# Router logits, a token transposition and an output product cut to the column tiles of the matmuls around them

## The reference

```python
h = _L0_tok_ref(x)
h = h + _L0_attn_ref(_layernorm(h), Wq, Wk, Wv, Wo)
h = h + _L0_ffn_ref(_layernorm(h), sW1, ..., gW, gb)

def _L0_attn_ref(q_input, Wq, Wk, Wv, Wo):        # 8 heads of 64
    qkt = jnp.einsum('bifh,bjfh->bijh', q, k)
    attn = jax.nn.sigmoid(qkt * SCALE)
    wv = jnp.einsum('bijh,bjfh->bifh', attn, v)
    return jax.nn.relu(wv.reshape(b * s, f * h) @ Wo)

def _L0_ffn_ref(x, ...):                            # 4 experts, the best 2 of each token
    all_out = _experts_mlp(x, eW1, eb1, eW2, eb2, eW3, eb3)
    shared = _shared_mlp(x, sW1, sb1, sW2, sb2, sW3, sb3)
    gates = jax.nn.softmax(x @ gW + gb, axis=-1)    # the router
    topv, topi = jax.lax.top_k(gates, TOPK)
    topw = jax.nn.softmax(topv, axis=-1)
    ...
```

## Time and profile before

| | |
|---|---|
| runs | 157.02, 158.77, 161.1 us; median 158.77 |
| the profiled execution | 158.76 us, of which the span from first to last instruction is 156.9 |
| busy share of the span | PE 93%, PEld 56%, DVE 71%, ACT 76%, POOL 35% |
| first and last scores of the part that matters | 81.38 us (step 48), 98.09 us (step 63) |

### The profile page before, as it was taken

How to read it: one execution, slowest core, us unless ns; L and a number is a source line. 1 busy time by engine, 2 the same in 40 slices (tenths; PEclk the granted TensorE clock), 3 DMA queues, 4 the chain that set the end, 5 groups by cost and what they waited for, 6 DMA issues and landing times.

```text
span 156.9 us, 6708 instructions
## 1 busy us (share of the span) xinstructions
PE 146.5 (93%) x2856; PEld 87.3 (56%) x2856; DVE 111.0 (71%) x282; ACT 119.3 (76%) x163; POOL 55.4 (35%) x102
## 2 busy tenths in 40 slices
PE   7999595998999999999999999999999999999990
PEld 2479532544456665656665656453566476576680
DVE  2396998998676958586763253879568987879680
ACT  3498992886888999999997989779738767857530
POOL 7000008879498473738265316376100000000000
PEclk9999659999999999999999999999999999999999
DMA  4390000156687496689589800101000010000112
GB/s 107 72 279 24 4 0 0 34 140 188 171 231 209 158 293 138 196 199 258 148 254 176 169 5 4 33 13 24 6 4 18 19 37 19 20 21 16 39 37 65
DMA packets 16734, 15.02 MB, mean 96 GB/s; under 512 B 4792, under 2 KB 15964, under 8 KB 16640
## 3 DMA queue, kind: packets, MB, share of 16 engines
q1 hardware_dynamic: 15888, 13.97, 34.0%
q10 hardware_dynamic: 816, 0.62, 1.3%
HBM read 9.06 MB, written 4.60 MB: 87 GB/s over the span
## 4 chain that ended last, share of the span: by engine, by line
PE 73%; DVE 7%; DMA 6%; ACT 6%; POOL 4%; issue 1%; POOLq 0%; DVEq 0%
PE ps L487 15%; PE ps L505 14%; PE ps L618 9%; PE ps L634 9%; PE ps L516 5%; DMA y_stage<-YP 4%; PE ps L676 4%; PE ps L644 3%; DMA YS<-y_stage 2%; PE ps L368 2%; PE ps L698 2%; PE ps L721 2%; PE ps L357 2%; PE ps L542 2%; POOL norm L1426 1%
## 5 line engine op out<-in xcount | busy, mean ns | idle before, releaser
L1315 ACT ACTIVATE probs<-ps 125x1000 f32<-125x1000 f32 x64 | 63.1, 1006 | 7.7 <-PE ps L487 3.3
L505 PE MATMUL ps<-probs,xn 124*32 124x250 f32 (+1 forms) x512 | 38.5, 375 | 0.3 <-ACT probs L1315 0.3
L487 PE MATMUL ps<-YS,XT 128*32 128x500 f16 x448 | 33.8, 375 | 1.1 <-DMA YS<-y_stage 1.1
L1333 ACT ACTIVATE area<-ps,wf 128x500 f32<-128x500 f32 x32 | 21.1, 672 | 7.7 <-PE ps L618 7.7
L940 DVE COPY ZS<-ps 128x250 f32<-128x250 f32 x32 | 13.2, 413 | 16.9 <-PE ps L505 16.9
L505 PEld LDWEIGHTS ps<-probs,xn 124*32 124x32 f32 (+1 forms) x512 | 15.3, 109 | 12.6 <-ACT probs L1315 1.2
L1347 ACT ACTIVATE area<-ps,wf 128x500 f32<-128x500 f32 x20 | 13.5, 676 | 4.7 <-PE ps L644 2.4
L634 PE MATMUL ps<-area,wf 128*64 128x500 f32 x64 | 16.3, 584 | 0.0
L516 PEld LDWEIGHTS ps<-outW,ZS 128*32 128x32 f32 (+1 forms) x512 | 10.7, 108 | 5.0 <-issue 0.6
L487 PEld LDWEIGHTS ps<-YS,XT 128*32 128x32 f16 x448 | 10.0, 96 | 5.5 <-DMA YS<-y_stage 2.1
L921 DVE CAST YP<-ps 128x500 f16<-128x500 f32 x14 | 9.5, 677 | 4.5 <-PE ps L446 4.1
(11 more groups left out here) (170 smaller groups left out, 263.2 us busy)
## 6 DMA issues: line engine op xcount, KB each, us to landing
YS<-y_stage SPq DMA_DIRECT2D x28, 250.0 KB, 4.2
y_stage<-YP SPq DMA_DIRECT2D x10, 250.0 KB, 3.8
wf<-wf_in SPq DMA_DIRECT2D x1, 648.0 KB, 5.8
y_stage<-YP SPq DMA_DIRECT2D x5, 125.0 KB, 4.6
tower_out<-res SPq DMA_DIRECT2D x5, 124.0 KB
wa<-wa_in SPq DMA_DIRECT2D x1, 512.0 KB, 5.1
y_stage<-YP ACTq DMA_DIRECT2D x3, 125.0 KB, 2.9
tower_out<-res SPq DMA_DIRECT2D x2, 112.0 KB
```

The lines of the kernel that those rows point to most:

```text
L487: last = mm(ps[k0:k1, 2 * (n % 2) + j, 0:TG].rearrange("p (h n) -> p h n", h=2), XT[:, g % 3, (2 * bb + cj) * P + k0:(2 * bb + cj) * P + k ...
L505: last = mm(ps[R * hh:R * hh + R, 4 + bb, half * TB:(half + 1) * TB], xn[0:keys, 4 * g + 2 * bb + cj, :], probs[0:keys, n % 3, hh, :], sta ...
L1315: fn(probs[:, n % 3].rearrange("p (j h) n -> p j (h n)", j=2), ps[0:P, 2 * (n % 2):2 * (n % 2) + 2, 0:TG], ACT.Sigmoid, scale=SCORE_SCALE) ...
L1333: fn(H1[:, g % 2, e, :], ps[:, n % 3, 0:TG], ACT.Relu, bias=wf[:, WF["b1"][0] + e:WF["b1"][0] + e + 1]).then_inc(l1_act, 1)
```

## The change

Four edits. The router's matmuls are cut along the token columns: tiles of 32 columns in the first router, of 64 in the second. The first router goes in eight pieces of two token tiles, behind steps 0, 1, 2, 7 of group 6 and 0, 1, 4, 7 of group 7. The transposition of the last group's tokens is cut in two 64-column parts for each token tile in the place of four of 32. Group 1's output product goes one token tile a step (t = 4 to 7). On DVE, `gate_logits(0)` moves behind `z_take(7, 2)`, since its input is now complete only in step 63.

```diff
-GATE_STEPS = tuple(8 * (NG - 2) + t for t in (0, 1, 2, 7))
+GATE_STEPS = tuple(8 * (NG - 2) + t for t in (0, 1, 2, 7, 8, 9, 12, 15))
...
-                    for c in range(4):
-                        last = nc.tensor.transpose(xt[R * c:R * c + R, i, 0:P], x2s[0:P, g % 2, i, R * c:R * c + R],
+                    for c in range(2):
+                        last = nc.tensor.transpose(xt[F * c:F * c + F, i, 0:P], x2s[0:P, g % 2, i, F * c:F * c + F],
...
-                    row = NB * r + i
-                    last = mm(ps[0:P, bank, 2 * i * E:2 * (i + 1) * E],
-                              X2T[:, row // 4, row % 4, 0:P],
-                              wg[:].rearrange("p k e -> p (k e)"), start=True, stop=True)
+                    row, wide = NB * r + i, F if r else R
+                    for q0 in range(0, P, wide):
+                        q1 = min(q0 + wide, P)
+                        last = mm(ps[q0:q1, bank, 2 * i * E:2 * (i + 1) * E],
+                                  X2T[:, row // 4, row % 4, q0:q1],
+                                  wg[:].rearrange("p k e -> p (k e)"), start=True, stop=True)
...
-                return {1: (6, 7), NG - 2: (3, 4, 5, 6), NG - 1: (2, 3, 5, 6)}.get(g, (3, 5, 6, 7))
+                return {1: (4, 5, 6, 7), NG - 2: (3, 4, 5, 6), NG - 1: (2, 3, 5, 6)}.get(g, (3, 5, 6, 7))
...
-                    first_tile = out_steps(g).index(t) * 4 // len(out_steps(g))
-                    if first_tile == 0 and g + 2 < NG:
+                    tile = out_steps(g).index(t)
+                    if tile == 0 and g + 2 < NG:
                         pe.wait_ge(xt_cp, g + 3)
-                    elif first_tile == 0:
+                    elif tile == 0:
                         pe.wait_ge(h2_done, g - 1)
-                    attn_out(g - 1, range(first_tile, first_tile + 4 // len(out_steps(g))))
+                    attn_out(g - 1, (tile,))
                 if n in GATE_STEPS:
                     i = GATE_STEPS.index(n)
-                    gates(0, slice(4 * i, 4 * i + 4))
+                    gates(0, slice(2 * i, 2 * i + 2))
...
                 z_take(g, 1)
                 if g == NG - 1:
-                    gate_logits(0)
                     add_attention(g - 1)
                     centre2(g - 1)
                 z_take(g, 2)
+                if g == NG - 1:
+                    gate_logits(0)
```

## The result

Over 22 runs the changed kernel takes 156.75 us (154.59 to 159.64), the kernel before 158.87 (157.02 to 161.56, 22 runs). The ratio is 0.985, 95% interval 0.981 to 0.988. That is faster, by less than the 2% that count, and where it was forecast: 156.6, in a range of 154.6 to 159.0.

The account below looks back on a forecast made before the run. TensorE was taken as the bound, with ACT setting group 7's pace before the change. Savings of 1.4 (first router), 0.53 (second router) and 0.2 (transposition) sum to 2.1 us off 158.76, giving 156.6, range 154.6 to 159.0.

Parts of the forecast that it names:

- The bound: Whole kernel: TensorE bounds it, busy 146.5 of 156.9 us; steps without a side piece are ACT's.
- First router: Groups 6 and 7: 32-column tiles save 1.0 in steps 48 to 50, 0.71 in step 55, less 0.29: 1.4 us.
- c: Price of one first-router piece of eight tile matmuls, taken as 0.11 us; saving 2.18 - 7c with the pause gone.
- the pause in step 55: TensorE's unexplained 0.38 us stop inside the old router's piece, taken as gone; if it returns, 1.05 us is saved.
- the piece in step 63: Last first-router piece, in group 7: stands ahead of a mix that waits for ACT, so costs nothing.
- Second router: Feed-forward: 32 matmuls on 64-column tiles take 0.6 us where the old run cost 1.13, saving 0.53.
- Transposition: Last group's tokens, feed-forward: 64-column tiles avoid running dry, saving 0.2 us, bounds 0 and 0.22.
- Hand-over: Attention to feed-forward: late logits cost nothing; as a rival, they eat up to 0.4 us, giving 157.0, chance 0.1.
- Group 1: Output product moved to steps 12 to 15: saves nothing; ACT's two pauses of 0.3 us go away.
- One after another: Rival, both routers: tile matmuls run serially at 28 ns each, giving 157.8 us; chance 0.2.
- Slower: Rival, both routers: small matmuls with loads cost 64 ns whatever the tile, giving 160.9 us; chance 0.08.
- another wait takes all of it: Rival: another wait in group 7 or 1 sets the end, time stays at 158.8 us; chance 0.1.

Follow-up runs that it names:

- only_ffn_tiles: Kernel before with only the second router and the last transposition on 64-column tiles; median 157.99 us, ratio 0.988 to the kernel before.
- only_group1: Kernel before with only group 1's output product spread over four steps; median 158.35 us, ratio 1.001 to the kernel before.
- changed_again: The changed kernel itself, unaltered, run again on a third chip; median 156.49 us, ratio 0.984 to the kernel before.
- only_first_router: Changed kernel with second router, last transposition and group 1 as before, first router still tiled in eight pieces; median 157.65 us, ratio 0.991 to the kernel before.
- logits_early: Changed kernel with gate_logits(0) back at its old place on DVE; median 157.07 us, ratio 0.999 to the kernel before.
- plain_copies: Changed kernel with the DMA transpositions of X2T replaced by plain copies of the same bytes; median 155.69 us, ratio 0.987 to the kernel before.
- no_reads: Changed kernel reading nothing of YS back from memory for groups 3 to 7; median 154.70 us, ratio 0.987 to the kernel before.
- half_reads: Changed kernel reading back only half of YS for groups 3 to 7; median 155.66 us, ratio 0.978 to the kernel before.

## Why the prediction was right, point by point

**The bound.** TensorE sets the pace of groups 1 to 6 and of the feed-forward: right. The 0.84 us taken from it in the feed-forward arrived in F (0.87), and ACT's idle times in group 1 were worth nothing.

**First router.** The mechanism was right, the price was not. With c = 0.05 instead of 0.11 the forecast's own formula, 2.18 - 7c, gives 1.83. But 0.38 of this was the pause in step 55, and pauses did not go; without it 1.45 is left. Measured, with the pauses of steps 51 and 55 taken out by the length of the steps around, A is 18.58 to 18.62 in three traces with the old router (before, only_ffn_tiles, only_group1) and 17.34 to 17.36 in five with the new one (changed, changed_again, only_first_router, logits_early, plain_copies): 1.26 less. (no_reads and half_reads, with 17.23 and 17.24, leave out reads too.) Steps 48 to 50 and 55 gave 0.39 each. The other 0.2 that the formula has too much are two terms: group 7 needed 7.08 and not the 6.98 of c = 0.05, as steps 56 and 57 lasted 0.96 and 0.92 where the two kernels with fewer reads have 0.90 or 0.91; and the piece in step 63, which was to cost nothing, cost 0.07 (2.35 from there to layer 1, for 2.28). Why steps 56 and 57 are longer is open.

So 1.4 forecast and 1.26 measured is in part luck: a piece too dear by half (0.4) and a pause taken as gone (0.38) cancelled, and two small costs were left out. Group 7 did become TensorE's, 7.08 us for the 7.16 forecast.

**Second router.** 0.50 for the 0.6 taken, 0.63 saved for 0.53. The pair of tile matmuls came at 0.031, as the 0.03 of the nearest rows had it; the allowance for longer loads was not needed.

**Transposition.** 0.21 saved, forecast 0.2. **Hand-over.** No cost, as forecast; the 1.05 us of logits_early show that its cover was thin in the other order. **Group 1.** Nothing, as forecast, though ACT's two pauses did not go away as it had said.

**The sum.** 1.26 + 0.63 + 0.21 = 2.1 us for the 2.1 forecast, and 2.1 measured between the medians (158.87 and 156.75). The ratio of 0.985 with its interval is 1.9 to 3.0 us.

**The rivals.** One after another: wrong, since a matmul costs 6 or 16 ns and not 28. The Trainium skill's rule in "TensorEngine Tiling (Array Packing)", Instruction Overhead, of about 60 cycles for every free dimension from 1 to 60, would have given 25 ns each (an estimate at 2.4 GHz). If it holds within a tile, four tiles side by side share it: 6 ns on four tiles and 16 on two are 25 and 31 for a matmul of each tile, so the trace agrees with the figure and not with the advice against tiling a dimension that is already small, where the price had been a load of the whole array. Slower: wrong, far from its 40 ns. Hand-over: wrong, as F is 50.93 in only_first_router and before alike. That another wait takes all of it: wrong for the medians, though the pauses did just that in the one trace.

## What to carry to other kernels

A small matmul on the whole array between column-tiled ones cost 0.06 us here, and each piece of such matmuls another 0.20 for running dry, ahead and behind: cut it to its neighbours' tiles even if it streams 8 columns, and don't mind four times as many instructions. Cut it for the tiles and not for the number of pieces: four and eight pieces were the same. And when an engine's order has a late consumer (the logits here), move its reader behind everything that does not need it, or a piece moved for free costs a microsecond at the next hand-over (1.05 in F of logits_early).

## What the runs showed that I had not expected

TensorE loses up to 1.5 us at a time at fixed places of its order, 256 instructions (125 or 126 matmuls) apart or a multiple, in some executions and not in others: at the seams of its instruction stream, whenever the packet with the next block has not landed 1.2 to 1.5 us ahead. In the traces of kernels with full traffic this took between 0.4 and 3 us of attention, as much as this whole change is worth. It is the best explanation I have for single runs of one kernel that lie 3 to 5 us apart, and that much is not shown, since only one run of each was traced. Two profiles of such a kernel should be compared step by step, with these stops taken out of both, before anything is said on a difference of 1%.
